# Sixty small warm-up matmuls in place of 28 larger ones: TensorE's program moved by 128 instructions

## What is computed

```python
def _L0_xattn_ref(x, cond, Wq, bq, Wk, bk, Wv, bv, Wo, bo):
    q, k, v = Wq x + bq, Wk cond + bk, Wv cond + bv      # (128 x 128) weights
    dots = jnp.einsum('bhdt,bhdtw->bhtw', qh, k_win) * scale   # 8 heads, window of 16 positions
    attn = jax.nn.softmax(dots, axis=-1)
    out = jnp.einsum('bhtw,bhdtw->bhdt', attn, v_win)
    return Wo out + bo
def _L0_ffn_ref(inputs, gate_w, lora_A, lora_B):
    ...
    weights, sel = jax.lax.top_k(gate_probs, TOP_K)      # 2 of 8 experts, rank 64
    for e in range(N_EXPERTS):
        y = x @ lora_A[e].T @ lora_B[e].T
        out = out + w_full[:, e:e + 1] * y
x = x + _L0_xattn_ref(_layernorm(x, axis=-1), ctx_4096, ...)
x = x + _L0_ffn_ref(_layernorm(x, axis=-1), ...)
```

## Time and profile before

| | |
|---|---|
| median of 3 runs | 1057.43 us (1052.64 to 1060.89) |
| profiled execution, its own time | 1057.9 us |
| its span | 1056.1 us |
| TensorE matmul busy | 1011.5 us (96%) |
| VectorE busy | 872.8 us (83%) |
| ScalarE busy | 582.5 us (55%) |
| GpSimd busy | 432.5 us (41%) |
| DMA engines, mean | 88 GB/s |

### The profile page before, as it was taken

How to read it: one execution, slowest core, us unless ns; L and a number is a source line. 1 busy time by engine, 2 the same in 40 slices (tenths; PEclk the granted TensorE clock), 3 DMA queues, 4 the chain that set the end, 5 groups by cost and what they waited for, 6 DMA issues and landing times.

```text
span 1056.1 us, 54652 instructions
## 1 busy us (share of the span) xinstructions
PE 1011.5 (96%) x24508; PEld 869.8 (82%) x24508; DVE 872.8 (83%) x1889; ACT 582.5 (55%) x812; POOL 432.5 (41%) x373
## 2 busy tenths in 40 slices
PE   6879999999999999999999999999999999999987
PEld 5768888888888888888888888888888888888866
DVE  3778888888888888888889888889888888888852
ACT  6666555556555556555555555556555555654420
POOL 7773434434434434343434343444343443443210
PEclk9899999999999999999999999999999999999998
DMA  7232333322333322223332223332233332222210
GB/s 271 78 80 86 83 84 103 103 66 81 82 83 103 103 81 71 76 84 103 103 85 71 84 83 91 103 103 58 87 84 83 103 103 73 76 81 64 64 41 40
DMA packets 157721, 92.47 MB, mean 88 GB/s; under 512 B 139728, under 2 KB 139856, under 8 KB 157520
## 3 DMA queue, kind: packets, MB, share of 16 engines
q1 hardware_dynamic: 157520, 89.25, 28.9%
HBM read 55.16 MB, written 16.78 MB: 68 GB/s over the span
## 4 chain that ended last, share of the span: by engine, by line
PE 87%; issue 5%; DVE 5%; ACT 2%; DMA 1%; POOL 1%; DVEq 0%; SPq 0%
PE bank_a L351 35%; PE bank_b L401 18%; PE bank_c L351 16%; PE bank_b L380 13%; PE bank_a L410 5%; DVE stats L815 1%; DMA raw<-x 1%; DMA prob_t<-ctx 0%; DVE h_sb L875 0%; DVE row_max L886 0%; DVE row_sum L900 0%; DVE pick L861 0%; DVE resid_pair L954 0%; POOL x_split L1120 0%; ACT x_split L688 0%
## 5 line engine op out<-in xcount | busy, mean ns | idle before, releaser
L401 PEld LDWEIGHTS bank_b<-prob_t,v_diag 64*64 64x64 f32 x4608 | 192.0, 134 | 50.3 <-issue 41.9
L401 PE MATMUL bank_b<-prob_t,v_diag 64*64 64x96 f32 (+2 forms) x4608 | 211.4, 239 | 12.6 <-issue 12.2
L351 PE MATMUL bank_a<-down_split,mid_split 128*128 128x264 f32 (+1 forms) x1536 | 213.7, 289 | 1.5 <-DVE mid_split L934 1.4
L351 PEld LDWEIGHTS bank_a<-down_split,mid_split 128*128 128x128 f32 x1536 | 193.4, 188 | 8.6 <-DVE mid_split L934 2.3
L1091 POOL TENSOR_TENSOR prob<-prob,row_inv 128x512 f32<-128x512 f32 x128 | 134.2, 1049 | 159.0 <-DVE row_inv L904 157.2
L351 PE MATMUL bank_a<-up_split,ht_split 128*128 128x512 f32 x768 | 196.6, 407 | 2.8 <-DVE ht_split L941 2.8
L380 PEld LDWEIGHTS bank_b<-k_sb,q_diag 32*32 32x32 f32 x16384 | 155.0, 105 | 43.9 <-issue 36.7
L380 PE MATMUL bank_b<-k_sb,q_diag 32*32 32x32 f32 x16384 | 170.6, 195 | 10.7 <-issue 6.7
L351 PEld LDWEIGHTS bank_a<-up_split,ht_split 128*128 128x128 f32 x768 | 142.8, 192 | 33.7 <-DVE ht_split L941 3.3
L1114 POOL TENSOR_TENSOR attn_split<-attn,attn_split 128x1024 fp32r<-128x1024 f32 x32 | 76.1, 2378 | 145.6 <-ACT attn_split L676 145.6
L913 DVE STREAM_TRANSPOSE prob_t<-prob 128x768 f32<-128x768 f32 x128 | 122.9, 961 | 0.9 <-POOL prob L1091 0.9
(11 more groups left out here) (79 smaller groups left out, 1316.2 us busy)
## 6 DMA issues: line engine op xcount, KB each, us to landing
v_diag<-v_t SPq DMA_DIRECT2D x128, 132.0 KB, 3.3
raw<-x SPq DMA_DIRECT2D x32, 512.0 KB, 4.5
resid_pair<-x SPq DMA_DIRECT2D x32, 512.0 KB, 4.0
out<-resid_pair SPq DMA_DIRECT2D x32, 512.0 KB, 4.3
raw<-ctx SPq DMA_DIRECT2D x30, 512.0 KB, 3.3
stage<-down_w SPq DMA_DIRECT2D x2, 528.0 KB, 10.6
q_diag<-up_w SPq DMA_DIRECT2D x2, 512.0 KB, 5.7
prob_t<-up_w SPq DMA_DIRECT2D x2, 512.0 KB, 7.2
```

Source lines behind the costliest of these rows:

```text
L351: return nc.tensor.matmul(dst, st[:, s, st_cols], mv[:, m, mv_cols], start=start and n == 0, stop=stop and n == 2)
L401: last = nc.tensor.matmul(bank_b[2 + m % 2][rows, lo * PW:hi * PW], value_blocks(b)[rows, n, :], prob_t[rows, at:at + (hi - lo) * KT], sta ...
```

## The change

The warm-up issues 60 matmuls with 32 columns in place of 28 with 128 columns. Each is two passes of two instructions, so 28 x 4 = 112 instructions become 60 x 4 = 240, and everything behind them stands 128 instructions later in TensorE's program. Nothing else differs; what is multiplied is zero and is not read.

```diff
@@ -478,11 +478,11 @@
                 pe.wait_ge(prob_zero, 1)
                 for n in range(matmuls):
-                    nc.tensor.matmul(bank_c[:, 0:P], prob[:, 0:P], prob[:, 0:P], start=True, stop=True)
+                    nc.tensor.matmul(bank_c[0:KT, 0:KT], prob[:, 0:KT], prob[:, 0:KT], start=True, stop=True)
 
             def head(b0, b1, b2, b3):
 
-                warm_up(28)
+                warm_up(60)
                 first_masks()
```

## The result

The changed kernel takes 1047.28 us in the median of 13 runs (1040.44 to 1049.37), the kernel before 1059.16 us in 13 runs beside it (1052.44 to 1061.68). The ratio is 0.988, 95% interval 0.9861 to 0.9898: 1.2% faster. The profiled execution of the changed kernel took 1048.8 us at a span of 1047.0 us, against 1057.9 and 1056.1 us.

A forecast was written before the change was run, and what follows sets the result against it. TensorE bounds the kernel, stalling on late instruction packets. 1056.1 - 12.0 + 1.2 + 0.3 = 1045.6 us of span, plus 1.8 around it, 1047.4, less 0.5 to the median: 1047.0 us; 8 in 10 from 1042 to 1055.

The forecast's parts named there:

- What "issue" is: TensorE's unexplained waits at L401 (12.2 us) and L380 (6.7 us): the next packet of 256 instructions is not there.
- Rival C: The shift does nothing, as the place in the packets is not what stalls TensorE: 1057 us, chance 0.07.
- Which interval decides: Shortest time between packet borders in a step grows from 3.03 to 3.38 us, against packets taking 3.3 to 4.1.
- a to b, b to c, c to d, d to e and e to f: Five of a step's six intervals between packet borders after the change: 4.9, 7.5, 4.4, 3.7 and 6.8 us.
- f to a: Interval from the step's last scores chunk to the weighted chunk after project_o: 3.38 us, 3.7 with VectorE's wait.
- The floor of a step: A step without the stall takes 8.93 + 22.08 = 31.0 us against 31.43, gaining 12.0 us in 28 steps.
- The cap: VectorE's chain from the logits to h_sb is late next, so 0.35 us of each stall cannot be gained.
- New stalls: Late packets from c to d and d to e, under DMA traffic: 0.04 us a step, 1.2 us in all.
- (e): Packet border 87 passes into the scores chunk after the down(0) halves; may be 0.35 us late for nothing.
- The head: Before the steady steps: two stalls of about 2 us for one of 1.97; net +0.3 us, bounds -2 and +3.
- Rival A: Borders as forecast, but stalls of 0.2 to 0.4 us a step or the head's +3 swallow the gain; chance 0.25.
- rival B: Slower: a packet queues behind the loads of resid and x, +1.3 us a step, 1094 us; chance 0.08.

The follow-up runs named there:

- the kernel with both moves: Changed kernel with VectorE's first_norm(later) moved behind weigh_experts and inner_lo(old) ahead of scores_shift(cur, 3): 1036.75 us.
- 28 small: Changed kernel with 28 warm-up matmuls of 32 columns in place of 60, so no shift: 1060.27 us, ratio 1.0004 to the kernel before.
- the two with VectorE's moves: Kernel before with VectorE's first_norm(later) moved behind weigh_experts: 1058.65 us; with inner_lo(old) also ahead of scores_shift(cur, 3): 1060.35 us.

## Why the prediction was right

The forecast was 1047.0 us; 1047.28 was measured. Its steps:

*What "issue" is.* Right. A shift of 0 and of 256 restore the time, 48 and 192 make it worse, and the stalls stand where the count puts them (87, 121 and 249 passes in). Each such wait ends some 1.4 us after a packet of q8 has landed. Rival C falls, and with it, for this chip and program, the rule that the prediction took from the Trainium skill (Runtime: NRT & Kernel Launch, section "Instruction fetch mechanics"), 128 KiB of room for TensorE and a crossing that is mostly hidden. The trace shows a packet of 256 instructions, as that section says, and stalls of up to 2.5 us at single crossings of a step.

*Which interval decides.* Partly wrong, without harm to the sum. The lengths were right: a to b, b to c, c to d, d to e and e to f last 4.80, 7.56, 4.43, 3.66 and 6.78 us in the trace of after. But the prediction put the gain down to the shortest interval growing from 3.03 to 3.38 us, f to a, against a packet that takes 3.3. By the record of q8 the length is not what saves it. In the kernel before, the packet that the short interval waits for starts 1.2 us after the border that opens it, on average; in the changed kernel the one for f to a starts 0.4 us ahead of border f, behind the six passes of project_k on 128x512, and has landed 2.8 us or more before it is used. The tightest is d to e, 1.9 us on average and 1.35 us at the one stall. The "4.07 us" of a packet under a burst of data was 1.75 us until it started, 0.93 us of transfer and 1.39 us from its landing to TensorE's next pass.

*The floor of a step.* Right: 8.93 + 22.08 = 31.0 us forecast, 30.97 us in the step shown, 31.07 us on average. (The 8.93 of the sum is the 8.91 of the trace.) Over 28 steps (31.43 - 31.07) x 28 = 10.1 us, against 12.0 - 1.2 = 10.8 in the sum.

*The cap.* Right in kind and in size: VectorE's chain from the logits is 8.91 us long before and after, and taking it apart gives the missing time, though only with a second move. The wait for h_sb was forecast at 8 to 10 us. The matmul's 12.2 us include the two longest, 2.5 us together, which stand in the kernel with both moves too; the 26 others are 9.7 us, 0.37 us each. "Something late right behind" was more than one result. Only the first was named.

*New stalls.* 1.2 us were put down. The profiled execution shows 1.24 us in one step at (e) and little else.

*The head.* This is the term that was mis-sized: +0.3 us forecast, while the first transposes of h_sb came 2.1 us later (92.96 against 90.8). Some of it is not the shift's. The norm of batch 1 began 1.6 us later, since its x landed later (22.2 against 20.6 us), in a stretch that TensorE does not pace. In the other kernels with a shift of 128 the x landed at 21.3 to 21.5 us. The stalls were 0.95 and 2.15 us for one of 1.97, and 1.11 us ahead of project_o, about what was forecast. How much of the 2.1 us the shift causes was not separated by a run of its own. The kernels together say that most of it goes with the shift: those without a shift (before, 28 small, and the two with VectorE's moves) have their first transposes of h_sb at 90.7, 92.1, 91.3 and 92.8 us, those with a shift of 128 at 92.9, 93.5, 93.9 and 93.7, which is 1.8 us later on average. It was within the bounds given.

*Against the median.* The profiled execution gained 9.1 us and the medians 11.9; with runs of one kernel spread over 9 us, agreement of the forecast to 0.3 us is luck beyond what the terms deserve.

Rival A (1050 to 1056) and rival B (1094) did not come. B's price was not measured in steady form; what fits its mechanism is seen once, at 210.28 us, with a packet 2.80 us in its transfer.

## What to carry to other kernels

When TensorE's program is unrolled and full of small matmuls, count instructions between "issue" waits: if they come out as multiples of 256, the instruction stream is late, and the place of the borders in the work matters. Where a step is a whole number of packets long, a handful of idle instructions ahead of it sets all borders at once; scan a few shifts, and place the borders so that each interval holds large matmuls and begins behind wide ones (512 columns here). Before reckoning the gain, look for what is late just behind the stall, as here it kept half; and since any edit that adds instructions to TensorE moves these borders, a gain or loss of 1 to 5% of such an edit may have nothing to do with its purpose.

## What the runs showed of the hardware that I had not expected

A packet can be asked for while TensorE still has wide matmuls queued, and is then free even when the interval behind its border is very short: 1.32 us with no stall (shift of 48), where an interval of 3.03 us stalls by 0.3 to 1.2 us. Behind the passes of down(0) on 128x264 this did not happen: the interval of 1.41 us stalled by 1.7 us on average. From a packet's landing to TensorE's next pass it is 1.4 us. The granted clock fell to 0.50 behind 20 of 29 stalls of 0.75 to 2.54 us, and the one looked at cost another 1.2 us. And the longer warm-up of before had bought nothing: 28 small matmuls, 3.20 us by that run's timeline, gave the same time as 28 large ones in 9.16 us.
